# A transformer block on one core: another opening of the last stage, aggregated norm statistics, and the last two norms shared between ScalarE and VectorE

## The reference

```python
def _layernorm(x, axis=-1, eps=1e-05):
    m = jnp.mean(x, axis=axis, keepdims=True)
    v = jnp.var(x, axis=axis, keepdims=True)
    return (x - m) / jnp.sqrt(v + eps)

def attn(x):                       # 16 heads of 16, causal
    q, k, v = x @ wq + bq, x @ wk + bk, x @ wv + bv
    return softmax(mask(q k^T / 4)) v @ wo + bo

def ffn(x):                        # per sequence: the first token picks 2 of 8 experts
    idx = top_k(x[:, 0, :] @ Wr + br, 2)
    return sum over the two of (gelu(x @ W1[e] + b1[e]) @ W2[e] + b2[e]) / 2

x = x + _layernorm(attn(_layernorm(x)))
x = x + _layernorm(ffn(_layernorm(x)))
```

## Time and profile before

| what | us |
|---|---|
| median of 3 runs (2061.21 to 2065.99) | 2064.71 |
| the profiled execution | 2067.85 |
| its span | 2066.1 |
| busy in the span: PE, DVE, ACT, POOL | 1978.9, 1799.9, 1362.3, 316.4 |
| stage C, first projection to the end | 1709.9 to 2066.1 |

### The profile page before, as it was taken

One profiled execution on the slowest core, in us unless ns is written; L12 is line 12 of the kernel. 1 busy time (PEld: TensorE's weight loads), 2 busy tenths in 40 slices (PEclk: granted clock), 3 DMA queues, 4 the chain that ended last, 5 costly groups with the idle time before them and its releaser, 6 DMA issues.

```text
span 2066.1 us, 39584 instructions
## 1 busy us (share of the span) xinstructions
PE 1978.9 (96%) x15700; PEld 863.7 (42%) x15700; DVE 1799.9 (87%) x3564; ACT 1362.3 (66%) x1651; POOL 316.4 (15%) x366
## 2 busy tenths in 40 slices
PE   6999999999999999999999999999999996999997
PEld 3655333333333333333333333333333324666664
DVE  6876799999999999999999999999899917899873
ACT  3766657777777777777777777777777781333332
POOL 5333201010110101011100101011010104322000
PEclk9999989999999999999999999999999998999998
DMA  4877613150504224030513314050422034453220
GB/s 124 254 242 207 156 26 67 28 90 8 89 18 85 47 48 82 16 89 13 85 32 68 71 26 89 7 90 20 82 48 50 17 104 108 123 148 108 82 67 31
DMA packets 144651, 162.40 MB, mean 79 GB/s; under 512 B 52690, under 2 KB 118354, under 8 KB 144466
## 3 DMA queue, kind: packets, MB, share of 16 engines
q1 hardware_dynamic: 137554, 147.26, 30.5%
q0 software_dynamic: 6912, 12.61, 2.7%
HBM read 99.77 MB, written 59.77 MB: 77 GB/s over the span
## 4 chain that ended last, share of the span: by engine, by line
PE 79%; DVE 13%; ACT 4%; issue 1%; SPq 1%; DMA 1%; POOL 0%; ACTq 0%; DVEq 0%; POOLq 0%
PE b_psO L1103 25%; PE b_psS L1086 25%; PE b_ring L605 13%; PE a_psQK L888 6%; DVE b_pmax L621 3%; PE a_psV L900 3%; PE c_psH L1483 3%; PE c_psO L1496 2%; ACT b_prob L1050 2%; PE b_ring L603 1%; DVE c_attn L105 1%; DVE c_ln_f_stats L81 1%; DVE c_ln_x_stats L81 1%; PE c_psA L1453 1%; DVE c_x L1314 1%
## 5 line engine op out<-in xcount | busy, mean ns | idle before, releaser
L621 DVE TENSOR_REDUCE b_pmax<-b_ring 128x1 f32<-128x512 f32 (+4 forms) x2284 | 1336.6, 647 | 82.1 <-PE b_ring L605 65.1
L1050 ACT ACTIVATE b_prob<-b_psS 128x1024 f32<-128x1024 f32 (+3 forms) x1280 | 1085.1, 895 | 372.2 <-PE b_psS L1086 367.5
L1086 PE MATMUL b_psS<-g_qT,g_kT 64*128 64x512 bf16 (+6 forms) x5120 | 837.5, 349 | 10.0 <-ACT b_prob L1050 7.2
L605 PE MATMUL b_ring<-g_kT,g_qT 64*128 64x512 bf16 (+2 forms) x2500 | 717.5, 349 | 4.0 <-DVE b_pmax L621 2.6
L1103 PE MATMUL b_psO<-b_prob,g_v 128*32 128x512 f32 (+3 forms) x5120 | 597.3, 542 | 0.3
L1086 PEld LDWEIGHTS b_psS<-g_qT,g_kT 64*128 64x128 bf16 (+1 forms) x5120 | 296.6, 94 | 462.9 <-ACT b_prob L1050 343.4
L1021 POOL TENSOR_SCALAR_AFFINE_SELECT b_prob<-b_prob 128x512 f32<-128x512 f32 x256 | 164.5, 643 | 1321.1 <-ACT b_prob L1050 1320.9
L605 PEld LDWEIGHTS b_ring<-g_kT,g_qT 64*128 64x128 bf16 x2500 | 221.7, 94 | 236.3 <-DVE b_pmax L621 163.7
L603 PE MATMUL b_ring<-later,query_of 64*128 64x128 bf16 x988 | 192.4, 220 | 1.9 <-DVE b_pmax L621 1.3
L1103 PEld LDWEIGHTS b_psO<-b_prob,g_v 128*32 128x32 f32 x5120 | 103.6, 108 | 174.2 <-issue 132.8
L1483 PE MATMUL c_psH<-c_yT,c_w1e 128*128 128x512 f32 x256 | 121.0, 618 | 20.8 <-ACT c_hT L1408 20.7
(11 more groups left out here) (113 smaller groups left out, 1059.4 us busy)
## 6 DMA issues: line engine op xcount, KB each, us to landing
qk_parts<-a_parts SPq DMA_DIRECT2D x64, 384.0 KB, 4.6
g_qT<-qk_parts SPq DMA_DIRECT2D x184, 128.0 KB, 3.9
g_kT<-qk_parts SPq DMA_DIRECT2D x184, 128.0 KB, 5.2
out_sums<-b_outT SPq DMA_DIRECT2D x64, 256.0 KB, 2.6
v_ones<-a_v SPq DMA_DIRECT2D x16, 544.0 KB, 6.0
g_v<-v_ones SPq DMA_DIRECT2D x32, 272.0 KB, 5.3
a_x<-in_L_attn_x SPq DMA_DIRECT2D x16, 512.0 KB, 4.8
c_x<-in_L_attn_x SPq DMA_DIRECT2D x16, 512.0 KB, 6.9
```

Source lines behind the costliest of these rows:

```text
L605: ins_ = self.nc.tensor.matmul(to, groups.qT[own, g, h // 2, 0, t * P:(t + 1) * P], groups.kT[own, g, h // 2, 0, pc * CH:pc * CH + w], sta ...
L621: self.nc.vector.tensor_reduce(pmax[:, c % 2].rearrange("p (h t) n -> p h t n", t=TT)[:, heads[0]:heads[-1] + 1:2, qt, pc], bank[:, 0:k * ...
L1050: nc.scalar.activation(prob[:, j % PBUF, 2 * s:2 * s + 2, off:CH], psS[:, 2 * s:2 * s + 2, off:CH], ACT.Exp).then_inc(exp_done, 1)
L1086: ins_ = nc.tensor.matmul(psS[:, 2 * s + p, off:CH], kT[own, g, s, ab, kt * P:(kt + 1) * P], qT[own, g, s, ab, c * CH + off:(c + 1) * CH], ...
```

## The change

In the class LayerNorm, for all norms: the six small operations that made mean and variance out of the statistics are replaced by four `bn_aggr`, one for each token row of the tile, which give mean and variance directly.

For the norms of the attention's and the experts' output: VectorE writes the negated mean (`less`, 128x4), ScalarE adds it to the tile in place with four 128x256 operations right behind the root (`centre`), and VectorE multiplies by the inverse deviation and adds x or x1 in four 128x256 operations (`scale_and_add`). The 128x1024 additions L1314 and L1373 go. The part of `experts_end` behind the statistics is now a part of its own, `add_experts`, and stands behind `take_projection`.

The four filling steps go. Each engine has a `begin` of its own: the first chunk goes through projection, both norms and the transpose before the second projection, the routing of the first sequence comes behind the second projection, and the third projection waits for it. The fourth projection stands behind the first `hidden`.

```diff
     def variance(self, chain, src, var_done):
-        v, st, tmp = self.nc.vector, self.stats, self.tmp
+        v = self.nc.vector
         for t in range(TT):
-            last = v.bn_stats(st[:, t, :], src[:, t])
+            last = v.bn_stats(self.stats[:, t, :], src[:, t])
         chain.mark(last)
         chain.wait()
-        v.tensor_tensor(tmp[:, 0, :], st[:, :, 1], st[:, :, 4], ALU.subtract)
-        v.tensor_tensor(tmp[:, 1, :], st[:, :, 2], st[:, :, 5], ALU.add)
-        chain.mark(v.tensor_tensor(tmp[:, 2, :], st[:, :, 1], st[:, :, 4], ALU.add))
+        for t in range(TT):
+            last = v.bn_aggr(self.moments[:, t, :], self.stats[:, t, :])
+        last.then_inc(var_done, 1)
+    def negate_mean(self, v, var_done, count, less_done):
+        v.wait_ge(var_done, count)
+        self.nc.vector.tensor_scalar(self.less[:, :], self.moments[:, :, 0], -1.0, None, ALU.mult
+                                     ).then_inc(less_done, 1)
+    def root(self, eps, std_done):
+        self.nc.scalar.activation(self.std[:, :], self.moments[:, :, 1], ACT.Sqrt, bias=eps[:, 0:1]
+                                  ).then_inc(std_done, 1)
+    def centre(self, tokens):
+        for t in range(TT):
+            last = self.nc.scalar.activation(tokens[:, t], tokens[:, t], ACT.Identity, bias=self.less[:, t:t + 1])
+        return last
+    def invert(self, chain):
+        chain.mark(self.nc.vector.reciprocal(self.rstd[:, :], self.std[:, :]))
         chain.wait()
-        v.scalar_tensor_tensor(out=tmp[:, 3, :], in0=tmp[:, 0, :], scalar=float(D // 4), in1=tmp[:, 0, :],
-                               op0=ALU.mult, op1=ALU.mult)
-        chain.mark(v.tensor_scalar(self.mean[:, :], tmp[:, 2, :], 0.5, None, ALU.mult))
-        chain.wait()
-        v.tensor_tensor(self.var[:, :], tmp[:, 3, :], tmp[:, 1, :], ALU.add).then_inc(var_done, 1)
-
-    def root(self, eps, std_done):
-        self.nc.scalar.activation(self.std[:, :], self.var[:, :], ACT.Sqrt, bias=eps[:, 0:1],
-                                  scale=1.0 / D).then_inc(std_done, 1)
-
     def normalise(self, chain, src, dst):
-        v = self.nc.vector
-        chain.mark(v.reciprocal(self.rstd[:, :], self.std[:, :]))
-        chain.wait()
+        self.invert(chain)
         for t in range(TT):
-            last = v.tensor_scalar(dst[:, t], src[:, t], self.mean[:, t:t + 1], self.rstd[:, t:t + 1],
-                                   ALU.subtract, ALU.mult)
+            last = self.nc.vector.tensor_scalar(dst[:, t], src[:, t], self.moments[:, t, 0:1], self.rstd[:, t:t + 1],
+                                                ALU.subtract, ALU.mult)
+        return last
+    def scale_and_add(self, chain, centred, other, dst):
+        self.invert(chain)
+        for t in range(TT):
+            last = self.nc.vector.scalar_tensor_tensor(out=dst[:, t], in0=centred[:, t], scalar=self.rstd[:, t:t + 1],
+                                                       in1=other[:, t], op0=ALU.mult, op1=ALU.add)
         return last
...
         def steps(eng, step):
-            for c in range(NC):
-                step(-1, c)
             for b in range(B):
                 for c in range(NC):
                     step(b, c)
         def to_route(b, c):
-
-            if isinstance(b, int) and b == -1:
-                return 0 if c == NC - 2 else None
             return b + 1 if c == NC - 1 and not (isinstance(b, int) and b == B - 1) else None
...
             chunks.load_sums(sp, NPAIR - 1)
+            chunks.store_inverses(sp, NPAIR - 1)
+            load_next_x(2)
+            load_experts(0)
+            load_next_x(3)
             steps(sp, step)
...
                 ln_a.variance(Chain(v, chain_a, n * LN_MARKS), attn, var_a)
+                ln_a.negate_mean(v, var_a, n + 1, less_a)
             def add_attention(b, c, n):
                 v.wait_ge(std_a, n + 1)
-                ln_a.normalise(Chain(v, chain_a, n * LN_MARKS + LN_MARKS - 1), attn, attn).then_inc(norm_a, 1)
-                v.wait_ge(norm_a, n + 1)
+                v.wait_ge(centred_a, n + 1)
                 v.wait_ge(x_ld[c % 2], (b * 2 + c // 2 + 1) * 16)
-                nc.vector.tensor_tensor(x1[:, c], x_sb[:, c % 2], attn[:, :, :], ALU.add).then_inc(x1_done, 1)
+                ln_a.scale_and_add(Chain(v, chain_a, n * LN_MARKS + LN_MARKS - 1), attn, x_sb[:, c % 2], x1[:, c]
+                                   ).then_inc(x1_done, 1)
                 v.wait_ge(x1_done, n + 1)
                 ln_x.variance(Chain(v, chain_x, n * LN_MARKS), x1[:, c], var_x)
...
-                chain = Chain(v, chain_f, n * LN_MARKS)
-                ln_f.variance(chain, ffn, var_f)
+                ln_f.variance(Chain(v, chain_f, n * LN_MARKS), ffn, var_f)
+                ln_f.negate_mean(v, var_f, n + 1, less_f)
+            def add_experts(b, c, n):
+                p = c % 2
                 v.wait_ge(std_f, n + 1)
-                ln_f.normalise(chain, ffn, ffn).then_inc(norm_f, 1)
-                v.wait_ge(norm_f, n + 1)
-
+                v.wait_ge(centred_f, n + 1)
                 v.wait_ge(stored[p], 16 + (b * 2 + c // 2) * 16)
-                nc.vector.tensor_tensor(out_sb[:, p], x1[:, c], ffn[:, :, :], ALU.add).then_inc(out_done, 1)
+                ln_f.scale_and_add(Chain(v, chain_f, n * LN_MARKS + LN_MARKS - 1), ffn, x1[:, c], out_sb[:, p]
+                                   ).then_inc(out_done, 1)
+            def begin():
+                take_projection(0, 0, 0)
+                add_attention(0, 0, 0)
+                normalise_x1(0, 0, 0)
+                chunks.invert_sums(v, NPAIR - 1)
+                take_projection(0, 1, 1)
+                route(0)
+                add_attention(0, 1, 1)
+                normalise_x1(0, 1, 1)
+                take_projection(0, 2, 2)
+                add_attention(0, 2, 2)
+                normalise_x1(0, 2, 2)
+                take_projection(0, 3, 3)
             def step(b, c):
-                first = isinstance(b, int) and b == -1
-                if first and c == 1:
-                    chunks.invert_sums(v, NPAIR - 1)
                 for k, part in ((2, normalise_x1), (1, route), (3, add_attention), (0, experts_end),
-                                (4, take_projection), (2, route)):
+                                (4, take_projection), (0, add_experts)):
                     which = ahead(b, c, k)
+                    if b == c == 0 and part is normalise_x1:
+                        continue
                     if part is route:
-                        if to_route(b, c) is not None and (k == 2) == first:
+                        if to_route(b, c) is not None:
                             route(to_route(b, c))
                     elif which:
                         part(*which)
...
@@ -1419,19 +1455,30 @@
             def root_attn(b, c, n):
                 act.wait_ge(var_a, n + 1)
                 ln_a.root(consts.eps, std_a)
+                act.wait_ge(less_a, n + 1)
+                ln_a.centre(attn).then_inc(centred_a, 1)
             def root_ffn(b, c, n):
                 act.wait_ge(var_f, n + 1)
                 ln_f.root(consts.eps, std_f)
+                act.wait_ge(less_f, n + 1)
+                ln_f.centre(ffn).then_inc(centred_f, 1)
             def step(b, c):
                 order = ((0, gelu), (3, root_attn), (3, root_x1), (0, root_ffn), (2, copy_y))
                 for k, part in order:
                     which = ahead(b, c, k)
-                    if which:
+                    if which and not (b == c == 0 and part is gelu):
                         part(*which)
             act.sem_inc(gelu_done, 2)
+            for c in range(2):
+                root_attn(0, c, c)
+                root_x1(0, c, c)
+                copy_y(0, c, c)
+            root_attn(0, 2, 2)
+            gelu(0, 0, 0)
+            root_x1(0, 2, 2)
             steps(act, step)
...
-                if c == 3:
+                if n == 2 or c == 3:
                     pe.wait_ge(idx_done, b + 1)
...
-                pe.wait_ge(a_read, n + 3)
+                pe.wait_ge(a_read, n + 3 if b > 0 else 2)
...
+            def begin():
+                project(0, 0, 0)
+                turn_y(0, 0, 0)
+                project(0, 1, 1)
+                score_experts(0, 0)
+                project(0, 2, 2)
+                turn_y(0, 1, 1)
+                hidden(0, 0, 0)
+                project(0, 3, 3)
+                outer(0, 0, 0)
             def step(b, c):
-                first = isinstance(b, int) and b == -1
-                order = ((0, hidden), (1, score_experts), (0, outer), (2, turn_y), (4, project))
-                if first:
-                    order = ((4, project), (2, turn_y), (2, score_experts))
-                for k, part in order:
+                for k, part in ((0, hidden), (1, score_experts), (0, outer), (2, turn_y), (4, project)):
                     which = ahead(b, c, k)
```

(5 more changed lines are left out.)

33 lines of the change are left out of this document (17 added, 16 removed).

## The result

The changed kernel takes 2080.29 us (median of 5 runs, 2076.12 to 2084.68) against 2064.71 us (5 runs, 2058.71 to 2067.07) for the kernel before: a ratio of 1.0069, 95% interval 1.0048 to 1.0091. It is slower by 15.6 us; the forecast was 10.1 us slower. The profiled execution took 2080.32 us with a span of 2078.6, against 2067.85 and 2066.1.

What follows compares the result with a forecast made beforehand. TensorE, VectorE and the ScalarE round trip lay within 0.8 us per step; the change would make the round trip the bound. Opening 2.1, twelve steps 4.7 and end 3.3 gave +10.1 us: 2074.8, eight-in-ten range 2056 to 2086.

Steps and rivals of the forecast that it cites:

- the opening: Stage C from first bias addition to first eviction: earlier routing gains 3.3 us, longer chain of single chunks gives more back, +2.1.
- the twelve steps: Stage C between the opening and the last three steps: 237.4 us against 232.76, so +4.7.
- The loop through ScalarE: Round trip from gelu to next gelu in stage C: 18.83 us, bounding the step, 0.7 above TensorE.
- the collisions at the sequence starts: GpSimd's multiplication falls among VectorE's four scalings in two sequences' first steps: 2.1 us each, 4.2.
- those in the routing: GpSimd's multiplication falls among the routing's operations in the routing step: 0.5 us twice, 1.0.
- the three slow products: Hidden products on TensorE at a lowered clock behind late steps and the first: 1.3 us each, 3.9.
- Rival 4: The collisions miss at the sequence starts and the clock holds: no change, 2065.7 us; chance 0.13.
- The end and the rest: Last three steps, without projection: +1.1 us each, +3.3; behind the last eviction 0.
- Stage A: First norm, issued at about 8.8 us, still waits for GpSimd's second memset, so TensorE starts no sooner: 0.
- rival 3: Stage A: the first norm gets between the memsets, TensorE starts up to 7.1 us sooner: 2067.7 us; chance 0.09.
- Rival 1: ScalarE's four take 1.0 us, so TensorE keeps the pace at 18.11: -9.3, 2055.4 us; chance 0.15.
- Rival 2: Dear aggregation, 0.20 us each: loop grows by 0.5 + 0.4 per step, 2088 us; chance 0.11.

Runs made afterwards that it cites:

- p2: The changed kernel with GpSimd's multiplication cut to one column per partition for chunks 4 to 15: 2077.14 us, ratio 1.0054.
- e4: The changed kernel with ScalarE's copy of the transpose moved ahead of the root of the experts' output: 2068.78 us, ratio 1.0017.
- e3: The kernel before with the new norms and its own opening: 2070.10 us, ratio 1.0024.
- e8: The kernel before with the new norms and its own opening, the second norm of a chunk one step later: 2037.75 us, ratio 0.9863.
- e1: The kernel before with `bn_aggr` alone in every norm: 2049.09 us, ratio 0.9917.
- e5: The changed kernel with the whole second norm one step later, its store ahead of the next experts' loads: 2083.51 us, ratio 1.0093.

## Why the prediction came out as it did

The direction and the main mechanism held. The size was short by 5.5 us by the medians. In the profiled executions the difference is 12.5 against 10.1, and the largest error of a term is the opening's, 6.7 us. That the twelve steps came out right is in part luck.

**The step.** The loop through ScalarE is the bound, as forecast: third products wait, VectorE idles ahead of the reciprocal, evictions are equally spaced. It is 19.31 us and not 18.83. By the offsets from the first gelu (forecast, then measured at 1800.37): end of ScalarE's four 8.27, 8.37; scaling 8.52, 8.68; statistics 9.94, 10.38; aggregation 11.38, 11.82; eviction 11.70, 12.12; root 14.84, 15.20; copy 16.53, 17.01; gelu 18.83, 19.31. So two prices were too low. The scaling with the addition takes 1.70 to its follower, where 1.42 was taken from an operation with one tensor input. ScalarE's four hold up the next operation by 1.61, where 1.48 was taken, and do so twice. `bn_aggr` was priced rightly: the follower begins 0.30 behind it, forecast 0.32. On ScalarE the estimate from the page was the better one: the Trainium skill, "ScalarE: Activation LUTs", section "What ACT_TABLE_LOAD costs", gave 1.69 us for the four, and the rows have 1.69 to 1.71.

**The additions to it.** The forecast's twelve steps were 237.4, measured 235.97, and this is errors that cancel. The step was 0.48 longer, 5.8 in all. Against that, the collisions at the sequence starts (4.2) did not come, those in the routing came, 1.8 us each, and cost nothing (1.0 was forecast), and two of the three slow products did not come (2.6); the first step was 1.9 over the others where 1.3 was forecast. A sequence's start is 20.07, the step and 0.76 for `c_b2mean`, for which 0.78 was taken. The context loads at the two places took 5.83 and 5.20 us and not 9.14 as in the earlier trace rows, so the multiplication fell in VectorE's idle time there too. Rival 4 was right on the sequence starts and on most of the clock, and it didn't decide. The first step took 21.20, for the reason that the forecast had given it: its third and fourth products waited 5.21 us for the gelu and then took 5.56 instead of 3.70, 1.86 us more.

```profile
1779.94 5.56 PE L1530 MATMUL c_psH<-c_yT,c_w1e 128*128 128x512 f32 x8 [5.21 <-ACT c_hT L1444]
```

In p2, whose opening ended differently, they waited 3.63, took 3.70, and the step was 19.38. So a wait of 2.58 was followed by slow products in the earlier trace rows and one of 3.63 here was not: its length, from which the prediction told them, does not decide by itself.

**The opening.** Forecast +2.1, measured +8.8; this is the term of the sum that was most wrong. Counted from the first bias addition, forecast and measured: second projection 11.4, 12.6; routing done 22.7, 25.4; first hidden products 29.3, 35.1; root of the third chunk 41.3, 45.7; fourth chunk's scaling 48.4, 54.5; eviction 52.4, 59.1. Three things were missed. The first transpose, behind 10.99 us of idle, ran at a granted clock of 0.50, 1.2 GHz: 1.97 us against 1.04. A multiplication fell on the routing, where the prediction placed such collisions only in the steps. And it said that the loads "land sooner"; they were issued sooner, but behind a context load, and landed at 1748, which cost 2.93 us of waiting. So 5.8 of the 6.7 us lie ahead of the hidden products, and the last two of the three differ from trace to trace: e4's, where the multiplication missed the routing, has the hidden products at 31.9 and the eviction at 55.3, still 2.9 over the forecast. From there to the eviction the forecast had 23.1 and it took 23.9: a multiplication fell on the third chunk's scaling (2.67 us for 1.38), and the scalings with the addition were priced low. The comparison was uncertain too: the old order with the new norms opens in 45.8 (e3) or 48.7 (e8), less than the 50.3 from which the prediction counted.

**The end and the rest.** +3.3 forecast, +3.9 measured for the last three steps; 0 forecast and +0.3 measured behind the last eviction, where ScalarE's four take 1.70, the scaling with the addition 0.29 more than the scaling before, and the addition (1.26) and 0.38 of small operations go. Stage A: the first scaling did get in between the memsets at 8.55, as rival 3 had it, but the next one then stood behind the second for 7.09 us, the four ended at 17.02, and TensorE began 0.38 sooner instead of 7.

**The rivals.** Rival 1 fell: no step of the changed kernel is at 18.11, and e4 and e8 show that the loop was the reason. Rival 2 fell: e1 with the aggregation alone is faster. The page "Perfetto Trace Analysis" of the Trainium skill, section "Optimizing Scalar/DVE Operations", suggests moving work to ScalarE when VectorE is saturated. The runs agree only with a condition: in the loop the move cost about 20 us (e3 against e1), outside of it the same work on the same engine is part of the shortest kernel of the study. Whether it gains anything there, no run shows, since none has the late place and the aggregation without it.

What stays open: how the 7 us between hidden and the first eviction divide, and how far e1's gain and the late place would add up without ScalarE's part; neither was tried.

## What to carry to other kernels

Before work moves to a less busy engine, ask whether that engine stands in the loop that sets the step, and put the work behind the instructions that the bounding engine waits for. In a queue that runs in order, whatever is delayed takes along what stands behind it: moving one store made TensorE wait 15 us for weights. A change of several parts should be timed part by part; here one part was worth -17 us and was hidden by two others at +20 and +12, taken in that order. And a difference of a few microseconds between two profiled executions is not yet the edit's: kernels with the same opening differed by 3.8 us in it.

## What the runs showed of the hardware

The aggregation isn't held up by a GpSimd operation, while a small operation right behind it is. The changed kernel's timeline:

```profile
1746.75 2.34 POOL L1308 TENSOR_TENSOR c_cc<-c_cc,c_inv 128x1024 f32<-128x1024 f32 x1 [6.96 <-DMA c_inv<-inverse_sums]
1746.98 0.38 DVE L85 BATCH_NORM_AGGREGATE c_ln_a_moments<-c_ln_a_stats 128x2 f32<-128x6 f32 x4
...
1747.39 1.72 DVE L91 TENSOR_SCALAR c_ln_a_less<-c_ln_a_moments 128x4 f32<-128x4 f32 x1
```

Four aggregations take their usual 0.38 us inside the multiplication; the multiplication by -1 of four values, 0.17 elsewhere, takes 1.72 and ends with it. The norm of the kernel before had six small operations at such places, and one of them took 1.47 us at 1735.11 instead of 0.17.

A DMA of 1 KB took 5.8 us to land when it was issued just behind four context transfers of 256 KB on another queue, and 2.9 when it was not; 9.5 in e5, behind four such transfers, a store and a load of x.

The scaling with the addition, 256 columns with two inputs from the chip's memory, is 480 ns each and 1.67 for four, against 1.38 for four with one such input. It still saves 0.98 us of VectorE (1.42 and 1.26 to their followers for scaling and addition apart, 1.70 together), but in the changed kernel VectorE had idle time to spare.
